# Four PSUM banks for the second head's scan output, and quarter units of the input projection moved around it and behind the first head's prefix sums

## The reference

```python
dt = jax.nn.softplus(dbc[:, :, 0]); B_t, C_t = dbc[:, :, 1:1 + S], dbc[:, :, 1 + S:]
dt, B_t, C_t, x_h = (gather by perm, per head)
h = exp(dt * A) * h + dt * B_t * x_t          # step over 1024 tokens
y_t = einsum('bhds,bhs->bhd', h, C_t)         # + D * x
y = gather(y_h, inv) * jax.nn.silu(gate) + res
```

## Time and profile before

| | |
|---|---|
| median of three runs | 1782.38 us (1779.83 to 1783.09) |
| the profiled execution | 1799.47 us |
| its span, mean granted TensorE clock | 1797.7 us, 0.986 |
| TensorE (PE) busy | 1702.6 us, 95% |
| VectorE (DVE) busy | 1148.6 us, 64% |
| ScalarE (ACT) busy | 892.4 us, 50% |
| GpSimd (POOL) busy | 412.0 us, 23% |

### The profile page before, as it was taken

The page is one execution under the profiler, slowest core; times in us unless marked ns, Lnnn a source line. Parts: engine busy times, 40 slices in busy tenths (PEclk is TensorE's granted clock), DMA queues, the critical chain, the costliest instruction groups (busy, mean ns, idle before and its releaser), DMA issues.

```text
span 1797.7 us, 24269 instructions
## 1 busy us (share of the span) xinstructions
PE 1702.6 (95%) x8725; PEld 944.7 (53%) x8725; DVE 1148.6 (64%) x2232; ACT 892.4 (50%) x1091; POOL 412.0 (23%) x423
## 2 busy tenths in 40 slices
PE   4689899999999999999999999999999999999988
PEld 3255554555545555456545565455554565555643
DVE  6879585656754666546865568555675467652675
ACT  4657354555255544455634644455535554545442
POOL 0303402134022321132220430213302232113220
PEclk9789999999999999999999999999999999999999
DMA  6203410233112331132301341023311233113201
GB/s 204 90 0 105 137 33 18 89 106 130 39 50 74 109 103 39 72 99 90 96 20 71 123 138 37 18 90 112 123 39 66 76 97 104 33 48 100 70 24 47
DMA packets 124077, 140.22 MB, mean 78 GB/s; under 512 B 52259, under 2 KB 101475, under 8 KB 123950
## 3 DMA queue, kind: packets, MB, share of 16 engines
q1 hardware_dynamic: 109902, 103.18, 18.0%
q0 software_dynamic: 12288, 34.68, 5.8%
q10 hardware_dynamic: 1760, 0.71, 0.2%
HBM read 78.52 MB, written 60.01 MB: 77 GB/s over the span
## 4 chain that ended last, share of the span: by engine, by line
PE 75%; DVE 9%; issue 5%; DMA 4%; ACT 3%; another core or an unknown queue 2%; POOL 2%; SPq 0%; DVEq 0%; POOLq 0%; ACTq 0%
PE bank L1599 71%; POOL rows L482 1%; PE bank L1767 1%; PE bank L1825 1%; DVE bn L915 1%; DMA rows<-d_y,rank 1%; DMA d_y<-buf_b 1%; PE bank L1902 1%; DVE res L1262 1%; DVE res L1260 1%; POOL d_scan L465 1%; DMA rows<-d_scan 1%; DMA x_even<-in_x 1%; ACT res L645 1%
## 5 line engine op out<-in xcount | busy, mean ns | idle before, releaser
L1599 PE MATMUL bank<-buf_a,win_hi 128*128 128x512 f16 x1536 | 461.5, 382 | 8.3 <-DVE buf_a L987 8.1
L1599 PE MATMUL bank<-buf_a,win_lo 128*128 128x512 f16 x768 | 293.2, 382 | 0.0
L1599 PE MATMUL bank<-buf_b,w_hi 128*128 128x512 f16 x960 | 288.3, 382 | 2.3 <-DVE buf_b L987 2.3
L1599 PEld LDWEIGHTS bank<-buf_a,win_hi 128*128 128x128 f16 x1536 | 150.7, 99 | 183.6 <-issue 13.6
L465 POOL DMA_INDIRECT d_scan<-rows,rank x128 | 125.5, 980 | 345.9 <-ACT rows L650 303.3
L1599 PE MATMUL bank<-buf_b,w_lo 128*128 128x512 f16 x480 | 183.0, 381 | 0.0
L1599 PE MATMUL bank<-buf_a,w_hi 128*128 128x512 f16 x576 | 171.3, 379 | 1.8 <-DVE x_odd L1230 1.7
L482 POOL DMA_INDIRECT rows<-d_y,rank x128 | 124.5, 973 | 136.9 <-DMA d_y<-buf_b 98.9
L1599 PEld LDWEIGHTS bank<-buf_b,w_hi 128*128 128x128 f16 x960 | 93.9, 99 | 112.3 <-DVE buf_b L987 3.0
L1599 PEld LDWEIGHTS bank<-buf_a,win_lo 128*128 128x128 f16 x768 | 75.7, 99 | 92.2 <-issue 2.8
L1599 PE MATMUL bank<-gate,w_out 128*128 128x512 f32 x256 | 120.3, 603 | 1.1 <-DVE gate L1339 1.1
(11 more groups left out here) (254 smaller groups left out, 3163.9 us busy)
## 6 DMA issues: line engine op xcount, KB each, us to landing
rows<-d_scan SPq DMA_DIRECT2D x16, 1092.0 KB, 5.7
d_y<-buf_b SPq DMA_DIRECT2D x64, 256.0 KB, 2.2
work<-in_x SPq DMA_DIRECT2D x24, 512.0 KB, 4.5
d_gram<-rows SPq DMA_DIRECT2D x32, 260.0 KB, 2.5
x_even<-in_x SPq DMA_DIRECT2D x16, 512.0 KB
x_odd<-in_x SPq DMA_DIRECT2D x16, 512.0 KB
out_x<-x_even SPq DMA_DIRECT2D x16, 512.0 KB, 2.6
out_x<-x_odd SPq DMA_DIRECT2D x16, 512.0 KB, 2.6
```

The source lines that it names most:

```text
L1599: return eng.matmul(out, lhsT, rhs, start=start, stop=stop, skip_group_check=True, **kw)
```

## The change

- Head 1's output gets a bank for each of its quarters: 3, 4, 0 and 6 (`y_bank`). TensorE waits for no eviction between them; ahead of the third it waits for the last state update (`h_st`), since banks 0 and 6 held the states' increments. Head 0 keeps two banks and its waits.
- Of the 6 quarter units ahead of the 1x1 matmul and head 1's output, the last three (of unit 22) go behind the output, ahead of the y transposes. ACT evicts unit 22 behind head 1's output in place of ahead of it.
- Of the 16 quarter units ahead of head 0's sums, the last two (of unit 17) go behind the sums: 14 ahead, 8 behind. ACT's order stays there.

```diff
+        y_bank = ((3, 4, 3, 4), (3, 4, 0, 6))
...
                 def scan_y(h, j):
                     wait(eng, "y_mm", m, 4 * h + j + 1)
-                    act(yscan[:, h, 2 * j:2 * j + 2, :], ps[3 + j % 2][:, :].rearrange("p (c d) -> p c d", c=2),
+                    act(yscan[:, h, 2 * j:2 * j + 2, :], ps[y_bank[h][j]][:, :].rearrange("p (c d) -> p c d", c=2),
                         ACT.Copy).then_inc(s["y_ev"], 1)
...
                 scan_factors(1)
-                filler(3)
+                filler(2)
                 for j in range(4):
                     scan_y(1, j)
+                filler(1)
                 y_high(m, 0)
...
                     gn_sum(m + 1, 0)
-                filler(4)
+                piece(14)
...
                         wait(eng, "m_ev", m, 2 * h + 2)
-                        if j >= 2:
+                        if h == 0 and j >= 2:
                             wait(eng, "y_ev", m, 4 * h + j - 1)
-                        out = ps[3 + j % 2][:, (c % 2) * DH:(c % 2 + 1) * DH]
+                        if h == 1 and j == 2:
+                            wait(eng, "h_st", m, 7 * HEADS)
+                        out = ps[y_bank[h][j]][:, (c % 2) * DH:(c % 2 + 1) * DH]
...
                 scan_sums(0)
-                piece(6)
+                piece(8)
                 factor_rows(0, 0)
...
-                piece(6)
+                piece(3)
                 wait(eng, "w_maxr", m, 2 * ROUNDS + 3)
                 mm(bound_all, const("ones")[0:1, :], y_bound[0:1, 1:2], True, True).then_inc(s["w_maxb"], 1)
                 scan_y(1)
+                piece(3)
```

## The result

The changed kernel took 1791.96 us (median of five runs, 1790.57 to 1795.6) against 1782.38 us before (five runs, 1779.83 to 1783.09): ratio 1.0059, 95% interval 1.0045 to 1.0072. It is slower by 9.6 us, 0.5%. The forecast was no change, 1782.4 us. The profiled execution took 1791.96 us, span 1790.1 us.

What follows compares the result with a forecast made beforehand. TensorE carries 75% of the chain that ends last, so time moves only with its waits. 3.7 us lost and 3.7 gained summed to no change, 1782.4 us (chance 0.50), range 1775.5 to 1789.5.

Steps and rivals of the forecast that it cites:

- a difference of a few us carries over one to one: Whole sum: profiled execution, 1799.47 us, is 0.96% above the timed median; differences of a few us apply unchanged.
- the four on which the argument rests: TensorE's waits: factor transposes 9.1 us, third quarter of second head's output 5.2, second y transpose 2.0, gathered rows 5.6; together 21.9.
- Part 1: Two quarter units moved behind the first head's sums: 3.7 us lost (bounds 2.4 gained, 11.0 lost).
- The wait that the two quarter units were to fill stays: Before the first head's factor transposes, third image: the 0.67 us wait remains, ended by ACT in place of VectorE.
- The second term, the masks: Before the first head's sums, third image: masks end at 588.90, sums begin at 589.12, 0.2 us to spare.
- Late completions: Behind the first head's sums: ACT sees unit 17 complete only when the scatter ends, exp 0.77 us later, four images.
- rival A: Unit 17's completion is seen at once: Part 1 gains 2.4 us, net 6.1 gained, 1776.3 us; chance 0.22.
- Rival B: Unit 17's completion is seen one scatter step later in every looped image: net 7.3 us lost, 1789.7 us; chance 0.20.
- Part 2: Second head's output: four banks, three quarter units moved behind it; 3.7 us gained (bounds 1.9 lost, 12.3 gained).
- The bound: Before the small matmul ahead of the second head's output: new wait for VectorE, 1.08 us per image, 8.6 over eight.
- Rival D: The new 1.08 us wait isn't there because VectorE's chain moves ahead: up to 8.6 us gained, 1774 us; chance 0.05.
- Rival C: Unhidden table change: exp 1.38 us later in looped images and last, 9.7 us on top, 1792 us; chance 0.03.

Runs made afterwards that it cites:

- part 1 alone: Kernel before with only two quarter units of unit 17 moved behind head 0's sums; 1796.34 us, ratio 1.0071.
- the kernel before traced again: The kernel before, unchanged, run again with a new trace; 1783.31 us, ratio 1.0009, profiled execution 1782.44 us.
- part 2 alone: Kernel before with only four banks for head 1's output and three quarter units moved behind it; 1780.05 us, ratio 0.9983.
- the second time: The changed kernel, unchanged, run again beside the kernel before on the same chip; 1791.62 us, ratio 1.0040.
- twelve later traces: Traces after the first: the unchanged kernel before, the changed kernel's two and nine of other versions; no single time.
- four ahead: Kernel before with four banks, four quarter units ahead of the small matmul and two behind the second head's output; 1775.67 us, ratio 0.9960.
- one quarter unit: Kernel before with one quarter unit of unit 17, not two, moved behind the first head's sums; 1791.35 us, ratio 1.0054.

## Why the prediction was wrong

**The step that failed** is the sentence of the sum that takes the profiled execution for the usual one: "a difference of a few us carries over one to one". That execution lay 17 us above the usual one, its waits didn't carry over, and two of the four on which the argument rests stand in it alone. In the earlier trace rows, 9.1 us at L1825 were 2.0 in an ordinary execution (first image alone), and 5.2 us between the quarters were nothing; those for the DMA (5.6, in fact 6.2) and for the eviction at L1902 (2.0) were real.

**Part 1.** "The wait that the two quarter units were to fill stays" held in its arithmetic of ACT: eviction, load and exp came in the foreseen 0.20, 0.80 and 1.30 us. But there was no wait to stay. The 0.6 us listed at L1827 in each image from the second on is all new. The second term, the masks, was given as "enough, with 0.2 us to spare"; that was read in one image of the delayed execution. The same trace has less room elsewhere: 0.74 us in the first image (masks end at 152.11, sums start at 152.85) and 0.98 in the last, where 1.30 are needed. In the ordinary one the sums have 0.06 to 1.1 us of room, and 1.30 us earlier is too early in each: 4.5 us after the change, 7.7 with part 1 alone. So the second failed step is a term put at nothing. Forecast 3.7 us lost, measured 12.7, outside the bound of 11.0.

**Late completions.** I took 0.77 us of delay for unit 17's completion. It was seen at once, 0.20 us after the next matmul began. So rival A had the mechanism, and its sign of a wait near 0.6 us was met. Its time, 6.1 us gained, was wrong, since it too counted from waits that weren't there. Rival B needs late completions and falls.

**Part 2.** The forecast of 3.7 us gained was near the 3.0 measured, by terms that missed in both directions: the banks gave 0 and not 5.2; the DMA's wait gave 6.2 for 5.6 and the eviction's its 2.0. The bound came as foreseen: from the end of the three quarter units (626.12 + 1.94 = 628.06) to the small matmul at 629.12 are 1.06 us, against 1.08, of which the list shows 0.89 as idle, 7.2 over eight images. The listed waits add to 7.2 - 6.2 - 2.0 = 1.0 us gained only. Most of the other 2 us is in what a wait costs beyond its listed idle time (below). The stores and the gather were to "come 1.8 us earlier"; it was 1.0: the gather starts 639.95 - 626.02 = 13.93 us after the bounds' transpose, against 14.92 in the kernel before traced again (637.91 - 622.99); in the delayed execution it was 641.97 - 625.98 = 15.99, so the 1.8 was counted from a gather that was itself 1.1 us late. With 1.0 us the rows are still in time. Rival D falls: VectorE's chain didn't move.

**Rival C.** The Trainium skill (ScalarE: Activation LUTs, What ACT_TABLE_LOAD costs) gives about 1.28 us for a load and about 1.38 us for a drain. The load is exposed now, and the rows agree with 1.28; exp follows at 595.06, 0.02 us after the load ends, and the transposes come by the sum of the rows without any drain. Rival C's 1792 us was met by the number alone, not by its cause.

**The sum.** By the ratios, part 1 alone lost 12.7 us and part 2 alone gained 3.0, 9.7 together; the change lost 10.5 and, the second time, 7.1. The waits of the changed kernel against those of the kernel before traced again: masks + 4.5, transposes + 3.7, bound + 7.2, DMA - 6.2, eviction - 2.0, L1547 + 1.1, which is 8.3 of 9.5 us of span. The other 1.2 us aren't settled one by one. They hold terms of both signs; one of them is 1.7 us of waiting in the last layers (L1601 for VectorE's L989), which the second trace of the same kernel doesn't have.

## What to carry to other kernels

Before reading waits from a trace, put its own time beside the timed runs. If it is 1% off and the effects sought are 0.3% each, its waits are no base, and the ones that look strangest (a completion seen long after the matmul) are the first to doubt. A filler moved from one wait to another changes two arrivals and what the other engines have to do between them: ask of each unit moved which engine evicts it and what stands behind that eviction. Room that one image shows is not the room of all: read it in each. And where a transfer hangs on the stage whose filler is moved, try the sizes on both sides; here the best stood one quarter unit from the one chosen.

## What the runs showed of the hardware

- **One kernel, two patterns of completion.** In an execution of 1799.47 us VectorE started on the sums 1.09 us after TensorE's next unit had begun, and ACT on a finished unit 3.0 us after; in the next trace of the same kernel, 1782.44 us, it was 0.27 and 0.11 us. Of the twelve later traces only one has any completion event over 0.3 us late, a single one of 1.07. What sets it off stays open; no run here brings it about. That it goes with GpSimd's indirect DMAs was a guess of the prediction; these run in the same places in all traces, so they alone don't cause it.
- **A wait costs more than its listed idle time.** The y transposes show it best: from their start to the first matmul of the output projection the kernel before, traced again, takes 638.77 - 633.97 = 4.80 us with a listed wait of 0.25, the changed one 642.29 - 637.95 = 4.34 with none, so that wait is worth 0.46 us. At the factor transposes of part 1 alone the units end at 594.03 + 8 x 0.648 = 599.21 and the transposes begin at 599.99, 0.78 us with 0.62 listed. So 0.16 to 0.21 us go with each of these waits beyond what is listed. In the same way the wait for the gathered rows in the kernel before is 644.75 - 643.96 = 0.79 us with 0.64 listed, and the bound's is 1.06 - 0.09 = 0.97 with 0.89 listed, as that place has a gap of 0.09 us without a wait too. For part 2 that makes 0.21 + 0.15 - 0.08 = 0.28 us per image, 2.2 us in all.
- **The rows of the masks are sometimes late.** In four images, each of another trace, of the 96 of the twelve later traces, the sums waited 1.7 to 2.6 us for the masks, behind the reading of the rows in scan order (L1482 waiting for the DMA). It is rare enough to make no term, but it is why room ahead of the sums is worth having.
- **Such a wait can cost TensorE its clock.** In two of these four images (2.57 us idle in part 1 alone, 1.96 us in the changed kernel's second trace) the granted clock was half for a stretch behind it, and sums to transposes took 1.7 us longer than in the same place otherwise (10.01 for 8.32, 10.10 for 8.40). In the other two (1.9 us with four ahead, 1.7 us with one quarter unit) it stayed at full speed.
